# Three transformer layers behind local attention: the exponential's rounding as a two-input instruction, and the statistics of the second and fourth LayerNorm in other steps

## What is computed

```python
x = layernorm(x + local_attention(x))            # ln1, first half of the kernel
x = layernorm(x + int8_linear(x))                # ln2
x = layernorm(x + linear_attention(x))           # ln3
x = layernorm(x + ternary_ffn(x))                # ln4

def linear_attention(x):                         # 16 heads of 64
    q, k, v = x @ wq + bq, x @ wk + bk, x @ wv + bv
    Q, K = elu(q) + 1, elu(k) + 1
    KV, Ksum = sum_s(K * v), sum_s(K)
    return gelu((Q * KV / (Q * Ksum + 1e-6)) @ wo + bo)

def ternary_ffn(x):                              # hidden 1024, weights ternary
    h = bitlinear(x, w_fc) + gate * (x @ v.T @ fast_b.T @ u.T)
    return bitlinear(relu(h) ** 2, w_proj)
```

## Time and profile before

| | us |
|---|---|
| median of 3 runs | 3318.77 |
| lowest and highest | 3311.44, 3319.60 |
| the profiled execution | 3316.87 |
| its span in the trace | 3315.1 |

### The profile page before, as it was taken

The page is one execution under the profiler, slowest core; times in us unless marked ns, Lnnn a source line. Parts: engine busy times, 40 slices in busy tenths (PEclk is TensorE's granted clock), DMA queues, the critical chain, the costliest instruction groups (busy, mean ns, idle before and its releaser), DMA issues. The chain is left out here.

```text
span 3315.1 us, 70305 instructions
## 1 busy us (share of the span) xinstructions
PE 3037.6 (92%) x21167; PEld 2509.0 (76%) x21167; DVE 2469.6 (74%) x6865; ACT 2161.4 (65%) x5664; POOL 1651.5 (50%) x2222
## 2 busy tenths in 40 slices
PE   5999999999999999999999995989899889999886
PEld 4888788788778778778778873777777777777774
DVE  5877877787787687687687776777777777777774
ACT  4766666666666576576576573677777777777774
POOL 3655555555555455465465563244444444454444
PEclk9999999999999999999999997999999999999999
DMA  2000000000000000000000012000000000000000
GB/s 78 8 14 21 9 14 21 9 14 21 9 14 21 9 21 14 9 21 14 15 15 14 8 33 83 7 13 8 20 13 14 14 14 14 14 14 13 7 14 20
DMA packets 50150, 58.70 MB, mean 18 GB/s; under 512 B 2848, under 2 KB 47920, under 8 KB 49472
## 3 DMA queue, kind: packets, MB, share of 16 engines
q1 hardware_dynamic: 47056, 51.78, 4.9%
q10 hardware_dynamic: 2672, 1.87, 0.2%
HBM read 36.86 MB, written 16.78 MB: 16 GB/s over the span
## 5 line engine op out<-in xcount | busy, mean ns | idle before, releaser
L577 POOL TENSOR_SCALAR a_ex<-a_ex,a_rc 128x384 f32<-128x384 f32 (+1 forms) x1024 | 531.2, 532 | 752.9 <-DVE a_rc L489 752.6
L386 ACT ACTIVATE a_ex<-a_sm,a_nm 128x384 f32<-128x384 f32 (+1 forms) x1024 | 572.5, 560 | 101.5 <-DVE a_nm L482 98.5
L482 DVE CUSTOM_DVE_ANT_0 a_sm<-sc,a_mask,a_rn 128x384 f32<-128x384 f32 (+1 forms) x1024 | 531.5, 544 | 49.0 <-PE sc L267 46.9
L392 ACT ACTIVATE a_pt<-tp 128x256 f32<-128x256 f32 (+1 forms) x512 | 219.7, 429 | 305.0 <-PE tp L278 305.0
L236 PE MATMUL pj<-a_whi,a_xhi 128*128 128x384 f32 x1024 | 398.3, 389 | 2.1 <-DVE a_rb L460 2.1
L561 POOL TENSOR_TENSOR a_qr<-a_ra,a_rb 128x256 f32<-128x256 f32 x512 | 366.9, 731 | 37.4 <-DVE a_rb L460 37.1
L267 PE MATMUL sc<-a_kT,a_qT 64*128 64x384 f32 (+1 forms) x2048 | 346.6, 457 | 2.4 <-DVE a_nm L482 0.9
L236 PE MATMUL pj<-a_whi,a_xlo 128*128 128x384 f32 x1024 | 347.2, 339 | 0.0
L236 PE MATMUL pj<-a_wlo,a_xhi 128*128 128x384 f32 x1024 | 346.2, 338 | 0.0
L288 PE MATMUL qk<-a_pt,a_v 128*64 128x128 f32 x5120 | 316.5, 279 | 31.5 <-issue 21.2
L288 PEld LDWEIGHTS qk<-a_pt,a_v 128*64 128x64 f32 x5120 | 287.4, 139 | 68.6 <-issue 66.6
(11 more groups left out here) (202 smaller groups left out, 8036.1 us busy)
## 6 DMA issues: line engine op xcount, KB each, us to landing
a_xin<-x SPq DMA_DIRECT2D x16, 512.0 KB, 3.9
a_xres<-x SPq DMA_DIRECT2D x16, 512.0 KB, 3.8
y<-a_res SPq DMA_DIRECT2D x16, 512.0 KB, 3.1
b_y<-y SPq DMA_DIRECT2D x16, 512.0 KB, 3.8
out<-b_y SPq DMA_DIRECT2D x16, 512.0 KB, 2.9
a_xin<-wqkv SPq DMA_DIRECT2D x8, 256.0 KB, 2.7
a_pt<-wqkv SPq DMA_DIRECT2D x1, 1536.0 KB, 6.7
a_ot<-wqkv SPq DMA_DIRECT2D x1, 1536.0 KB, 10.3
```

The lines of the kernel that those rows point to most:

```text
L386: e.activation(ex[h][w][:, 0:width], sm[h][w % 2][:, 0:width], ACT.Exp, bias=nm[:, w, h:h + 1], scale=-1.0, accum_out=rs[:, w, h:h + 1]).t ...
L392: e.activation(pt[0][w][:, 0:width], TP[:, 0:width], ACT.Copy).then_inc(g['pt_act'], 1)
L482: e.tensor_tensor_reduce(out=sm[h][w % 2][:, 0:width], in0=SC[w % 2][h][:, 0:width], in1=mem['mask'][:, off:off + width], scale=rn[:, par, ...
L577: e.tensor_scalar(row, row, 0.0, rc[:, w, h:h + 1], ALU.add, ALU.mult).then_inc(g['exn_pool'], 1)
```

## The change

There are three edits, all in `run_layers`.

1. `dve_q`'s first instruction was a `tensor_scalar` with two immediates. It becomes a `scalar_tensor_tensor` whose second input is a new column `one`, repeated 512 times; the arithmetic is the same. `pool_begin` fills the column once.
2. `dve_stats` takes a half k and waits for that half's sum alone. ln4's halves stand in steps 1 and 2, behind `dve_q` and ahead of `dve_square`, where all of it was at the start of step 4; ln4's rstd on POOL goes from step 4 to step 3. ScalarE's `apply` of ln4 keeps its place in step 5.
3. ln2's halves stand in steps 4 and 5 at that same place, where all of it was in step 5. ln3 keeps its place; its two halves are issued one after the other, each with its own wait.

```diff
--- before.py
+++ after.py
@@ -1064,6 +1064,7 @@
         e.memset(mem['eps'][:, :], LIN_EPS)
         e.memset(mem['ln_eps'][:, :], math.log(LIN_EPS))
         e.memset(mem['unround'][:, :], -ROUND)
+        e.memset(mem['one'][:, :], 1.0)
         e.memset(mem['half'][:, :], -0.5)
         e.memset(mem['ones'], 1.0).then_inc(w['set_pool'], 1)
         e.wait_ge(w['set_pool'], 1)
@@ -1392,7 +1393,8 @@
     def dve_q(e, s, c):
         n = HC * s + c
         e.wait_ge(g['qe_act'], n + 1)
-        e.tensor_scalar(mem['eq'], mem['eq'], -1.0, 1.0, ALU.add, ALU.add).then_inc(g['qt_dve'], 1)
+        e.scalar_tensor_tensor(mem['eq'], mem['eq'], -1.0, mem['one'][:, 0:1].to_broadcast([P, S]), ALU.add,
+            ALU.add).then_inc(g['qt_dve'], 1)
         e.wait_ge(g['qt_dve'], n + 1)
         if due(n):
             e.wait_ge(g['ql_act'], n)
@@ -1435,9 +1437,9 @@
         e.tensor_tensor(bank_rows(mem['dn'][:, k, :]), bank_rows(D[k]), row_pair('psc'),
             ALU.mult).then_inc(g['p_dve'], 1)
 
-    def dve_stats(e, norm, added, s, rows):
-        e.wait_ge(g[added], 2 * s + 2)
-        norm.stats(e, s, rows)
+    def dve_stats(e, norm, added, s, rows, k):
+        e.wait_ge(g[added], 2 * s + k + 1)
+        norm.stats(e, s, rows, (2 * k, 2 * k + 1))
 
     def dve_step(e, b, c):
         kv, at = (kv_unit(b, c), at_unit(b, c))
@@ -1451,12 +1453,11 @@
                 dve_out_bias(e, b - 1, k)
         if c in (3, 4) and inside(b + 2):
             dve_int8_scale(e, b + 2, c - 3)
-        if c == 4 and inside(b - 3):
-            dve_stats(e, n4, 'y4_pool', b - 3, y3_rows(b - 3))
         if c == 5 and inside(b - 1):
             dve_gelu(e, b - 1, 1)
         if c == 6 and inside(b - 1):
-            dve_stats(e, n3, 'y3_pool', b - 1, y3_rows(b - 1))
+            for k in range(2):
+                dve_stats(e, n3, 'y3_pool', b - 1, y3_rows(b - 1), k)
         if c == 7 and inside(b + 3):
             dve_round(e, b + 3)
         if inside(kv[0]):
@@ -1477,8 +1478,10 @@
                 dve_gelu_inner(e, b - 1, k)
         if c == 4 and inside(b - 1):
             dve_gelu(e, b - 1, 0)
-        if c == 5 and inside(b + 2):
-            dve_stats(e, n2, 's2_pool', b + 2, y2_rows(b + 2))
+        if c in (1, 2) and inside(b - 3):
+            dve_stats(e, n4, 'y4_pool', b - 3, y3_rows(b - 3), c - 1)
+        if c in (4, 5) and inside(b + 2):
+            dve_stats(e, n2, 's2_pool', b + 2, y2_rows(b + 2), c - 4)
         if inside(b - 2):
             dve_square(e, b - 2, c)
         if c == 7 and inside(b - 1):
@@ -1543,7 +1546,7 @@
                 pool_down_sum(e, b - 3, k)
         if c in (3, 4) and inside(b + 2):
             pool_int8_sum(e, b + 2, c - 3)
-        if c == 4 and inside(b - 3):
+        if c == 3 and inside(b - 3):
             n4.rstd(e, b - 3)
         if c == 5 and inside(b - 1):
             for k in range(2):
@@ -1631,7 +1634,8 @@
         return stack.enter_context(nc.sbuf_tensor('b_' + name, shape, dt))
     mem = {k: sb(k, v) for k, v in dict(ring=[P, 11, S], y1=[P, TT, DIM], qf=[P, TT, DIM], ws=[P,
         DIM], bo=[P, DIM], bias=[P, DIM], psc=[P, DIM], g1=[P, 2, S], g2=[P, 2, S], half=[P, TT],
-        eps=[P, 1], ln_eps=[P, 1], unround=[P, 1], xs=[P, 2], top=[P, 2], gate=[P, 1], wst=[P, 4, FC], nbq=[P, HC],
+        eps=[P, 1], ln_eps=[P, 1], unround=[P, 1], one=[P, 1], xs=[P, 2], top=[P, 2], gate=[P, 1], wst=[P, 4,
+            FC], nbq=[P, HC],
         nbk=[P, HC], bq=[P, HC], bk=[P, HC], one_bq=[P, HC], one_bk=[P, HC], bv=[P, HC], su=[P, 2, HC], kv=[P, HC],
         kb=[P, HC], ki=[P, HC], cc=[P, HC], nc=[P, HC], **Norm.buffers('ln2'), **Norm.buffers('ln3'),
         **Norm.buffers('ln4')).items()}
```

## The result

The changed kernel takes 3339.65 us (median of 4 runs, 3338.64 to 3343.24) against 3315.53 us before in the same session: a ratio of 1.0075, 95% interval 1.0057 to 1.0092. It is slower by some 24 us, where the prediction said 3336 us, 19 us above the profiled execution's 3316.87 us. The profiled execution has a span of 3336.8 us.

The account below looks back on a forecast made before the run. TensorE carries the time; VectorE adds only where it releases a bank late. Terms of 1.31 us a round give 14.4 in eleven rounds; with other rounds and 2.2 of clock, 18.7 on 3316.87: 3336 us, range 3316 to 3350.

Parts of the forecast that it names:

- The bound of "never held": Rounding (L1395): never held by POOL, it takes 0.68 us for 1.37, so -0.69 us.
- the faster rival: Rounding: the repeated one is not read like a tensor, L1395 is not held; about 3289 us, chance 0.12.
- step 3: TensorE's v products there wait for the late square of step 2: +0.85 us a round, the largest term.
- step 7: VectorE runs without a gap and the last transposes wait for L1351: +0.27 us a round.
- Step 2: Its v products wait for step 1's square, late by ln4's statistics and the rounding: +0.18 us a round.
- the wait of step 4: TensorE's wait at the v products of step 4 grows from 2.27 to 2.4 to 3.0 us.
- between the ends: Slip through step 3 into step 4's wait: +0.40 us, between +0.1 (rounding ahead of L1524) and +0.73 (held again).
- The low branch: Step 3: rstd holds L1387, so the rounding slips in ahead of POOL's L1524; +0.1 us.
- Step 5: In full-speed rounds step 4's square, behind held rounding and ln2 pair, is some 0.35 us late: +0.15 us mean.
- Step 6: Its wait of 0.73 us shrinks: one ln2 pair leaves step 5, 0.66 less 0.27 for the rounding: -0.40 us.
- Step 0: Absorbs the rounding's 0.27 us since ScalarE ends later there; no change.
- The rounds at the start and the end: Rounds before and after: some 1 us, 0.27 in each of few waiting steps; b = 14 1.7, b = 2 0.1, end -0.7.

Follow-up runs that it names:

- e7b: The kernel before, its rounding a one-input instruction that also writes a running sum (accumulator), constants 0.0: 3291.80 us, ratio 0.9923.
- e3: The kernel before with ln2's statistics in two pairs, steps 4 and 5, ln4's all in step 4, old rounding: 3313.46 us, ratio 0.9996.
- e5: The changed kernel with the pairs of ln4 and ln2 statistics behind each step's square instead of ahead: 3312.43 us, ratio 0.9991.
- e12: The changed kernel with the statistics pairs behind the square and POOL's subtraction waiting for the rounding: 3283.66 us, ratio 0.9888.
- e11: The changed kernel with POOL's subtraction of each step waiting until the step's rounding is done: 3292.75 us, ratio 0.9928.
- e6: The changed kernel with the statistics pairs behind the square and the old one-input rounding: 3307.03 us, ratio 0.9976.
- e9: The changed kernel with the old one-input rounding, statistics pairs behind the square, and POOL's subtraction waiting for the rounding: 3256.85 us, ratio 0.9821.
- e8: The kernel before with POOL's subtraction of each step waiting until the step's rounding is done: 3280.01 us, ratio 0.9886.

## Why the prediction was right, and where not

**What held.** The rounding is held, ends 0.55 us behind POOL (predicted 0.55), and takes 0.68 us free; 67 of 128 are held (before, 74; with the rounding alone, 81). The bound of "never held" did not come true. The nearest run to it is e7b, 3292 us, with a rounding of 0.69 us that is never held but the statistics where they were; the faster rival said 3289, though its own terms, 26 and 6 us off 3316.87, give 3285. The two terms on which the forecast leaned were met, in step lengths: step 3 by +0.81 us (0.85 predicted), step 7 by +0.25 (0.27). Step 2 is +0.32 for 0.18. In the rows the wait of step 3 is 0.56 us where the prediction looked for about 0.9, and the wait of step 4 was to grow to 2.4 to 3.0 us and fell to 2.08.

**The sum by step**, predicted and measured change of a step's length in us, rounds 3 to 13 (step 4's predicted figure is its wait +0.40, L1364 -0.14, and 0.20 of clock):

| step | 0 | 1 | 2 | 3 | 4 | 5 | 6 | 7 | round |
|---|---|---|---|---|---|---|---|---|---|
| predicted | 0 | 0 | 0.18 | 0.85 | 0.46 | 0.15 | -0.40 | 0.27 | 1.51 |
| measured | 0.43 | -0.03 | 0.32 | 0.81 | -0.62 | 0.55 | -0.21 | 0.25 | 1.52 |

The round agrees, and in part by luck: step 4 is a miss of 1.1 us one way, steps 0, 5 and 6 one of 1.0 the other way.

- **Step 4** was the term that I took "between the ends", +0.40 for a range from +0.1 to +0.73. The low branch came: the rounding of step 3 slipped ahead of the subtraction by 0.04 us. But not for the reason given: rstd (L85 and L87) did not hold L1387; it kept POOL busy until the subtraction could start at 2688.95, and the rounding had started at 2688.91. And even the low branch was too high: in full-speed rounds the step shrank by 0.8 us. The wait fell by 0.19, so the wait for L1364, which is gone, must have cost more than its recorded 0.33 us.
- **Step 5**, +0.55 for +0.15: in the full-speed rounds the square of step 4, behind a held rounding and a pair of statistics, comes 0.80 us late, where I had made it 0.35. TensorE reached it earlier, since step 4 had become shorter.
- **Step 6**, -0.21 for -0.40: taking away the pair is worth 0.44 us (e3), not 0.66; and edit 1 alone costs this step 0.51 us, not 0.27. The two do not simply add in this step.
- **Step 0**, +0.43 for nothing: the clock. The prediction gave the clock a price for step 4 alone. After 1.54 us of idle time at the end of step 7 step 0 kept it; after 1.79 to 1.84 us it lost it in five rounds of eleven (and in e5, after the same, in none). The rounding alone loses twice as much here, 0.85 us, which is a part of why it was worse than the whole change.
- **The rounds at the start and the end** gave 8.8 us, where I had about 2. There the stages are fewer and VectorE is waited for in more of the steps. TensorE's wait for the square behind round 13 is 11.3 us in place of 8.6, and for the query 7.1 in place of 6.6; I had counted a few steps by 0.27 us.

So the mechanisms of edit 1 (held, and then twice as long) and of step 3 were right; the costs by step were in part mis-sized, and the closeness of the sum is partly chance. The 3.7 us by which the attention half ended earlier in the traced execution hide a further part: from the start of the layers on, the trace is 25.5 us longer, where the terms gave 18.7. By the parts, edit 1 alone costs 30 us where the prediction's terms gave it about 10, and the statistics gain 6 where the terms gave them at most 5. The rest of the forecast, 9 us or more, stood for edit 1 and the statistics hitting each other in steps 2 and 3. They do (e5 has no wait in step 3), yet the parts simply add: what step 3 loses, steps 4 and 0 give back against the rounding alone (12.19 to 11.05 and 11.65 to 11.23).

## What to carry to other kernels

Where VectorE and GpSimd work beside each other, look for VectorE instructions whose duration has two values, and ask for each which GpSimd instruction it ran beside: the short one, eight columns in 1.20 us, is as dear as the long one. The subtraction is not the only one: in step 5 of round 8 of the changed kernel L1388, 0.55 us otherwise, took 1.44 us beside POOL's L1514 and ended 0.28 us behind it. Ordering the two by a semaphore can cost less than letting them meet: one added wait gave 1.1% here, and 1.8% with the statistics behind the square. Put work that no one waits for behind the instruction that releases a bank, and add to the price of each tenth of a microsecond of idle time in TensorE the chance that the clock falls after it.

## What the hardware showed that I had not expected

- A second input that is one column repeated 512 times is held like a full tensor: 1.69 us beside POOL's subtraction, 0.69 us free.
- The form that writes an accumulator is not held (0.69 us beside the subtraction); the plain form with two immediates is (1.37 us, 0.41 free).
- The hold works both ways: POOL's subtraction took 1.81 us where VectorE's two-input instruction had started 0.04 us ahead of it, 1.30 us where POOL was first. The accumulator form does not slow it: all 128 subtractions of e7b took 1.27 to 1.31 us, also where VectorE had started 0.17 us ahead.
- The granted clock is not a function of the last idle time alone. In step 4 it fell in five rounds of eleven after 2.16 us (e12), in ten of eleven after the same 2.16 us (e11, with the statistics elsewhere), in three after 2.49 us (e6), in one after 1.88 us (e9), in five after 1.87 us (e8), in none after 1.62 us (e7b). These are counts of one execution each. A slow step 4 costs 1.0 to 1.6 us. What else decides it stays open; no run here was made for it.
